# Cross-attention and expert layer in float32 parts: x's normed rows turned by VectorE blocks and GpSimd DMAs instead of TensorE, both query products late in the batch

## The chip, the cores and the metric

One core of a Trainium2 chip runs the kernel. The metric is the device time of one execution in microseconds; the median of several runs is given. A profiled execution is one more run, with its own time.

## What is computed

For each of 8 batches, x has 512 rows of 256 and the context 1601 rows of 256. The first layer is a cross-attention whose scores go through a sigmoid, not a softmax:

```python
q = (layernorm(x) @ Wq.T).reshape(B, L, 16, 16) * 16 ** -0.5
k = (ctx @ Wk.T).reshape(B, -1, 16, 16)
v = (ctx @ Wv.T).reshape(B, -1, 16, 16)
scores = sigmoid(einsum('blhd,bshd->bhls', q, k))
x = x + einsum('bhls,bshd->blhd', scores, v).reshape(B, L, 256) @ Wo.T
```

The second is a feed-forward layer on layernorm(x): a gate picks, for each of 16 experts and each batch, the 64 rows with the highest gate weights; these go through the expert's gated unit and are added to their rows, and a shared expert runs on all rows.

## The kernel before

**Attention, batch by batch.** A batch has 16 heads, 512 queries and 13 tiles of 128 keys. Its work is cut into 4 quarters (two halves of the heads, two sets of four heads in each) of 13 key tiles: 52 quads a batch. A quad is two *score pairs* (`scores`, L1735: two matmuls of 48 rows by 512 queries into one of three score banks), each followed by one sigmoid over 1024 columns on ScalarE (L876), and one *weighted sum* (`weighted_sum`, L1765). The 48 rows of keys and queries are three copies of 16 (high and low parts of float32 numbers), stacked in the tiles `keys` and `queries`.

**Products beside the scores.** While batch b's scores run, the products for batch c = b + 1 are made: keys K (`key_product`, by half of the heads and chunk of 512 keys), values V, queries Q (`query_halves`, one for each half), and, for batch b - 1, the output product O and the gate product G. T are the two products that turn x's normed rows by TensorE transposes (`turned_halves`, L1594), after which VectorE copies them into the tiles `nt_hi` and `nt_lo` (`turned_rows`, L1161) that Q reads. A product takes one of the three score banks (G has a bank of its own), like a score pair.

**The order** on TensorE is written out by hand: the strings `OPENING` (batch 0), `EACH` (batches 1 to 6) and `CLOSING` (batch 7) give S (score pair), W (weighted sum) and T (the next entry of the list `beside(b)`). VectorE and SyncE walk through the same list. On VectorE, `beside_quad(b, q)` (L1275) puts further work after given quads q: x's layer norm for c (sums at 15, scale at 17, rows at 19), the norm of the residual rows of batch b - 1 at 12 and the split of the turned ones at 22.

**The way of the residual rows** (batch b - 1) to their turned parts does not go over TensorE: `turn_norm` (L1189) transposes 32x32 blocks of `norm` into `norm_blocks` in one VectorE instruction, `place_norm` (L759) on GpSimd's queue issues 16 DMAs that put the blocks in their places, into `norm` again, and `split_norm` (L1194) makes `nt_hi` and `nt_lo` of them. G reads the placed rows from `norm`.

**SyncE's queue** (L596 on, in the order of the list). After each key product: `write_keys` to DRAM. After the last key product of c, K of half 1, chunk 3: `stack_keys` for the first two quarters of c, twice six DMAs of 200 KB back from DRAM (L505), once the writes have landed. After Q of half 0: `stack_queries(c, 0)`, twelve DMAs of 64 KB from `query_parts` into `queries` (L522). At the first pair of the next batch: `stack_queries` of half 1, and the keys of the third quarter. After the second T: `load_x` for the batch after c (L538). The first score pair of a batch waits for all twelve DMAs of half 0 (`wait_queries`, L1756).

**GpSimd's queue** (L768): for each batch its four context loads (`load_ctx`), each when the buffer of two loads before has been split, and `place_norm`.

After the attention come 24 units of the feed-forward layer, which the diff does not touch, apart from six early products (U) beside batch 7's scores.

## Time and profile before

| | |
|---|---|
| median of 3 runs | 1309.55 us (1308.88 to 1310.62) |
| profiled execution | 1305.85 us |
| its span, first to last instruction | 1304.0 us |
| TensorE clock granted over the span | 0.999 of full |
| engines busy | TensorE 98%, ScalarE 76%, VectorE 56%, GpSimd 22% |
| attention batches (first sigmoid to next first) | batch 0 112.87 us, batch 4 109.08 us |

Line numbers (L876) are those of the kernel before. PE is TensorE, PEld its weight loads, DVE VectorE, ACT ScalarE, POOL GpSimd, SP SyncE; SPq and the like are an engine's instruction queue. Times are microseconds from the span's start, unless they are marked ns. The last column of most views tells how long the engine was idle just before, and what ended that.

### The profile page before, as it was taken

What the parts mean: (1) busy time and instruction counts of PE and PEld (TensorE: products, weight loads), DVE (VectorE), ACT (ScalarE), POOL (GpSimd) and SP (SyncE); (2) the same over time, 40 slices, a digit from 0 to 9 for tenths busy, and PEclk for the clock granted to TensorE, in tenths of its full rate; (3) what the DMA queues carried; (4) which work ended last, traced back from release to release, by engine and by line L of the source; (5) the groups of instructions that cost most, each with busy time, mean ns of one, the idle gap of its engine ahead of it and who ended that gap; (6) DMA issues with size and microseconds to landing.
All of it is one profiled execution on the core that took longest, in us unless ns stands there. A gap on an engine that the chain in (4) does not pass through costs nothing.

```text
span 1304.0 us, 25503 instructions
## 1 busy us (share of the span) xinstructions
PE 1283.8 (98%) x10200; PEld 772.1 (59%) x10200; DVE 732.5 (56%) x1377; ACT 985.3 (76%) x1148; POOL 286.9 (22%) x288
## 2 busy tenths in 40 slices
PE   8999999999999999999999999999999999999997
PEld 6445444444454544544444443336888888888887
DVE  6564475365266448437536633215558777777773
ACT  5888989998998899899999989996333455555553
POOL 3000030020002003002000200500001567677635
PEclk9999999999999999999999999999999999999999
DMA  7785973874776597387477549713543577777754
GB/s 215 179 188 126 139 184 111 125 162 133 130 139 166 118 137 171 113 131 148 149 129 140 127 93 156 169 34 114 195 130 110 181 201 192 188 192 190 192 109 49
DMA packets 118726, 190.82 MB, mean 146 GB/s; under 512 B 22448, under 2 KB 71600, under 8 KB 118608
## 3 DMA queue, kind: packets, MB, share of 16 engines
q1 hardware_dynamic: 98768, 155.21, 51.9%
q0 software_dynamic: 19648, 33.72, 12.4%
q8 instruction: 81, 1.33, 0.5%
q10 hardware_dynamic: 192, 0.26, 0.1%
q14 instruction: 37, 0.30, 0.1%
HBM read 108.43 MB, written 55.61 MB: 126 GB/s over the span
## 4 chain that ended last, share of the span: by engine, by line
PE 87%; issue 5%; DMA 2%; DVE 2%; ACT 2%; POOL 1%; SPq 0%; POOLq 0%; DVEq 0%; ACTq 0%
PE score L1839 19%; PE score L1751 18%; PE acc L1780 14%; PE misc L1780 13%; PE score L1857 9%; PE score L1566 5%; PE score L1580 5%; PE score L1589 2%; ACT probs L876 1%; PE score L1619 1%; PE score L1607 1%; DMA key_scr<-key_parts 1%; POOL norm L765 1%; DMA norm<-norm_blocks 1%; DMA ctx_raw<-ctx_t 1%
## 5 line engine op out<-in xcount | busy, mean ns | idle before, releaser
L876 ACT ACTIVATE probs<-score 128x1024 f32<-128x1024 f32 (+1 forms) x832 | 789.8, 1026 | 77.3 <-PE score L1751 70.6
L1751 PE MATMUL score<-queries,keys 48*128 48x512 f32 (+1 forms) x1664 | 312.2, 438 | 6.5 <-ACT probs L876 4.2
L1751 PEld LDWEIGHTS score<-queries,keys 48*128 48x128 f32 (+1 forms) x1664 | 139.1, 180 | 275.0 <-ACT probs L876 212.7
L1780 PE MATMUL acc<-probs,values 128*32 128x512 f32 (+1 forms) x1664 | 210.5, 601 | 0.0
L1780 PE MATMUL misc<-probs,values 128*32 128x512 f32 (+1 forms) x1664 | 205.8, 600 | 0.0
L1026 DVE TENSOR_REDUCE whole<-score 128x512 f32<-128x1024 f32 (+1 forms) x75 | 77.0, 1026 | 196.6 <-PE score L1566 119.6
L729 POOL DMA_DIRECT2D ctx_raw<-ctx_t x32 | 23.4, 733 | 642.6 <-DVE ctx_lo L1004 557.9
L801 POOL DMA_INDIRECT gathered<-norm_scr,gather_row x64 | 81.2, 1269 | 227.5 <-DVE gather_row L1374 212.2
L891 ACT ACTIVATE gelu<-score 128x512 f32<-128x512 f32 (+1 forms) x97 | 55.5, 580 | 84.6 <-PE score L1839 84.0
L814 POOL DMA_INDIRECT out<-result,add_row x64 | 106.6, 1666 | 48.4 <-ACT result L944 25.9
L1839 PE MATMUL score<-tok_hi,gu_hi 128*128 128x512 f32 (+1 forms) x388 | 117.0, 383 | 0.0
L1839 PE MATMUL score<-tok_lo,gu_hi 128*128 128x512 f32 (+1 forms) x388 | 116.2, 381 | 0.0
L1839 PE MATMUL score<-tok_hi,gu_lo 128*128 128x512 f32 (+1 forms) x388 | 116.2, 381 | 0.0
L1321 DVE TENSOR_TENSOR hidden<-gelu,score 128x512 f32<-128x512 f32 (+1 forms) x97 | 64.0, 664 | 92.6 <-PE score L1839 62.3
L899 ACT ACTIVATE hid_hi<-hidden 128x512 fp32r<-128x512 f32 (+1 forms) x100 | 61.0, 613 | 63.9 <-DVE hidden L1321 60.7
L1066 DVE TENSOR_REDUCE values<-score 128x512 f32<-128x1024 f32 (+1 forms) x52 | 59.3, 1141 | 71.7 <-PE score L1580 71.0
L1780 PEld LDWEIGHTS misc<-probs,values 128*32 128x32 f32 (+1 forms) x1664 | 40.7, 108 | 87.0 <-issue 76.6
L1780 PEld LDWEIGHTS acc<-probs,values 128*32 128x32 f32 (+1 forms) x1664 | 38.8, 108 | 77.0 <-issue 71.5
L1839 PEld LDWEIGHTS score<-tok_lo,gu_hi 128*128 128x128 f32 x388 | 71.8, 188 | 14.2
L1839 PEld LDWEIGHTS score<-tok_hi,gu_lo 128*128 128x128 f32 x388 | 71.8, 188 | 14.1
L1839 PEld LDWEIGHTS score<-tok_hi,gu_hi 128*128 128x128 f32 x388 | 70.2, 189 | 12.9 <-issue 0.8
L944 ACT ACTIVATE result<-score,add_w 128x256 f32<-128x256 f32 x60 | 23.6, 474 | 67.9 <-DVE add_w L1364 64.7
(257 smaller groups left out, 1626.2 us busy)
## 6 DMA issues: line engine op xcount, KB each, us to landing
keys<-key_scr SPq DMA_DIRECT2D x180, 200.2 KB, 8.0
key_scr<-key_parts SPq DMA_DIRECT2D x45, 512.0 KB, 8.3
gu_raw<-w_gu SPq DMA_DIRECT2D x17, 1024.0 KB
ctx_raw<-ctx_t POOLq DMA_DIRECT2D x24, 512.0 KB, 5.1
queries<-query_parts SPq DMA_DIRECT2D x186, 64.0 KB, 2.5
d_raw<-w_d SPq DMA_DIRECT2D x17, 512.0 KB
norm<-xn SPq DMA_DIRECT2D x224, 32.0 KB
xn<-x SPq DMA_DIRECT2D x8, 512.0 KB, 3.8
```

What stands on the lines that cost most here:

```text
L801: pool.indirect_dma_start(gathered[par][:, t, :], None, norm_scr[:, :], bass.IndirectOffsetOnAxis(ap=gather_row[par][:, t:t + 1], axis=0)) ...
L814: pool.indirect_dma_start(out[:, :], bass.IndirectOffsetOnAxis(ap=add_row[par][:, t:t + 1], axis=0), result[par][:, t, :], None, compute_o ...
L876: act.activation(probs[0:rows, (n + 1) % RING, 2 * pair:2 * pair + 2, :], score[SLOT[k]][0:rows, :, :], ACT.Sigmoid, scale=SCALE).then_inc ...
L899: act.activation(hid_hi[par][:, of, cols], hidden[:, f % 2, cols], ACT.Copy).then_inc(hid_hi_done, 1)
L1026: dve.tensor_reduce(whole[:, 0:n], score[SLOT[task]][:, :, 0:n].rearrange("p e s -> p s e"), AX_X, ALU.add).then_inc(halves_added, 1)
L1321: dve.tensor_tensor(hidden[:, f % 2, cols], gelu[:, f % 2, cols], of, ALU.mult).then_inc(hidden_done, 1)
L1566: mm = pe.matmul(bank[:, e, 0:n], W2[a][rows, WK, k, P * half:P * (half + 1)], parts_of_ctx(b, kc)[c][rows, k, 0:n], start=(j == 0 and k = ...
L1580: mm = pe.matmul(bank[0:n, e, D * i:D * (i + 1)], parts_of_ctx(b, kc)[a][rows, k, s0:s0 + n], W2[c][rows, WV, k, :], start=(j == 0 and k = ...
L1751: mm = pe.matmul(score[SLOT[k]][0:rows, g, :], keys[quarter % KEY_RING][of, pair, P * st:P * st + rows], queries[half][of, e, pair, :], st ...
L1780: mm = pe.matmul(sums_bank[n // NST % 2][32 * c:32 * (c + 1), :], values[b % 2][0:rows, st, half, c, :], probs[0:rows, (n + 1) % RING, c, ...
L1839: mm = pe.matmul(bank[:, f % 2, cols], (gu_hi, gu_lo)[a][slot][:, w, k, P * of:P * (of + 1)], (tok_hi, tok_lo)[b][par][:, k, cols], start= ...
L1857: mm = pe.matmul(d_bank[:, t2, D * (t % 2):D * (t % 2 + 1)], (hid_hi, hid_lo)[a][par][:, f, P * t:P * (t + 1)], (d_hi, d_lo)[b][slot][:, f ...
```

## The change

- T is gone, with `turned_halves`, `turned_rows` and their waits; batch 0's own two stay.
- x's normed rows of batch c are turned as the residual rows are: `turn_x` is one VectorE block transpose from `xn` into the tile `norm` (viewed as `x_blocks`), right after G has been copied out (in batch 0 after quad 30); `place_x` on GpSimd's queue puts the blocks into `xn` (viewed as `x_raw`) with 16 DMAs; `split_x` on VectorE makes `nt_hi` and `nt_lo` after quad 42 (batch 0: 40). Q waits for the split.
- GpSimd's queue is rearranged: `place_x(b)` stands after the first two context loads of the batch after it and before the third.
- SyncE loads the x of the next batch but one after Q of half 0 instead of after T.
- The list `beside` and the strings have a new order. The number of score pairs of the batch that stand before a product, in batches 1 to 6 (c = b + 1, half or chunk behind it):

| product | before | after | | product | before | after |
|---|---|---|---|---|---|---|
| T, first and second | 52, 60 | gone | | V chunk 2, two halves | 75, 78 | 68, 74 |
| V chunk 1, two halves | 44, 47 | 47, 50 | | K chunk 3, half 0 and 1 | 83, 83 | 79, 79 |
| K chunk 2, half 0 and 1 | 66, 72 | 59, 62 | | V chunk 3 | 86 | 80 |
| G of batch b - 1 | 70 | 72 | | Q half 0 (Q0), half 1 (Q1) | 63, 95 | 89, 92 |

In batch 0 the last K moves from 85 to 78, and Q0 from 68 to 86; Q1 stays at 95.

```diff
     if c < B:
         out += [("V", c, 0, 0), ("V", c, 0, 1),
                 ("K", c, 0, 1), ("K", c, 1, 1), ("V", c, 1, 0), ("V", c, 1, 1),
-                ("T", c, 0), ("T", c, 1), ("Q", c, 0), ("K", c, 0, 2)]
+                ("K", c, 0, 2), ("K", c, 1, 2), ("V", c, 2, 0)]
...
     if c < B:
-        out += [("K", c, 1, 2), ("V", c, 2, 0), ("V", c, 2, 1),
-                ("K", c, 0, 3), ("K", c, 1, 3), ("V", c, 3, 0), ("Q", c, 1)]
+        out += [("V", c, 2, 1), ("K", c, 0, 3), ("K", c, 1, 3), ("V", c, 3, 0), ("Q", c, 0), ("Q", c, 1)]
...
-EACH = ("SSWWSSTSWSSSWWSTSTSSWWSSTSSWSSSWWSSTSSWSSSWWSSTSWSSSWWSTSTSSWWSSSWWSSSWWSSTSWSSTSWSSSWWSTS"
-        "WSSSWWSSSWWSTSWSSTSWSSTSWSSSWTWSSTSWSSTSWSSTSWSSSWWSTTSSWSTSWSSSWWSSSWWSSTSWSSSWWSSSWWSS")
+EACH = ("SWWSSTSWSSSWWSTSTSSWWSSTSSWSSTSWSSTSWSSSWWSSSWWSSTSWSSSWWSSSWWSSTSWSSSWWSSSWWSSTSWSSTSWSSS"
+        "WWSSSWWSSTSWSSTSWSSSWWSSTSSWSSWTSSTSWSSSWWSTTSTSWSSSWWSSSWWSSTSWSSTSWSSSWWSSSWWSSSWWSS")
...
+        x_raw = xn[:].rearrange("p t d -> p (t d)").rearrange("p (k s) -> p k s", s=S)
+        x_blocks = norm[:].rearrange("p t d -> p (t d)").rearrange("p (j c) -> p j c", c=P)
...
             def load_x(b):
-                sp.wait_ge(misc_copied, COUNT["T", b - 1, KC - 1])
+                if b > 1:
+                    sp.wait_ge(x_split, b - 1)
+                else:
+                    sp.wait_ge(misc_copied, COUNT["T", 0, KC - 1])
                 sp.dma_start(xn[:], x_rows[b]).then_inc(x_in, 16)
...
                         elif task[0] == "Q":
                             if task[1] == 0 or task[2] == 0:
                                 stack_queries(*task[1:])
-                        elif task[0] == "T" and task[2] == KC - 1 and task[1] + 1 < B:
-                            load_x(task[1] + 1)
+                            if task[1] and task[2] == 0 and task[1] + 1 < B:
+                                load_x(task[1] + 1)
...
+            def place_x(b):
+
+                pool.wait_ge(x_turned, b)
+                for i in range(BLOCKS):
+                    for j in range(BLOCKS):
+                        pool.dma_start(x_raw[TURN * j:TURN * (j + 1), :, P * i:P * (i + 1)],
+                                       x_blocks[TURN * i:TURN * (i + 1), j::BLOCKS, :]).then_inc(x_placed, 16)
+
+            for kc in range(NCH - 1):
+                load_ctx(1, kc)
             for b in range(1, B):
-                for kc in range(NCH):
-                    load_ctx(b, kc)
+                load_ctx(b, NCH - 1)
                 if b >= 2:
                     place_norm(b - 2)
+                if b + 1 < B:
+                    load_ctx(b + 1, 0)
+                    load_ctx(b + 1, 1)
+                place_x(b)
+                if b + 1 < B:
+                    load_ctx(b + 1, 2)
...
+            def turn_x(b):
+                dve.wait_ge(xn_ready, b + 1)
+                if b == 1:
+                    dve.wait_ge(direct_written, 16 * len(DIRECT))
+                    dve.wait_ge(first_keys_in[1], STACK_DMAS)
+                else:
+                    dve.wait_ge(post_stored, STORE * (b - 1))
+                dve.transpose(x_blocks.rearrange("p j (t q) -> p t j q", q=TURN),
+                              xn[:].rearrange("p t (j q) -> p t j q", q=TURN)).then_inc(x_turned, 1)
+
+            def split_x(b):
+                wait_past(dve, nt_stored, STORE * (b - 1))
+                dve.wait_ge(x_placed, PLACE_DMAS * b)
+                for k in range(KC):
...
+                    dve.tensor_copy(hi, raw).then_inc(split_step, s.up())
+                    dve.wait_ge(split_step, s.now())
+                    last = dve.tensor_tensor(lo, raw, hi.bitcast(F32), ALU.subtract)
+                last.then_inc(x_split, 1)
...
+                if b == 0 and q == 30:
+                    turn_x(1)
+                if b + 1 < B and q == (40 if b == 0 else 42):
+                    split_x(b + 1)
...
                         copy_out(which)
+                        if which == ("G", b - 1) and b + 1 < B:
+                            turn_x(b + 1)
...
                 elif kind == "Q":
+                    if b:
+                        pe.wait_ge(x_split, b)
                     mm = query_halves(task[2], bank)
...
-                elif kind == "T":
-                    pe.wait_ge(xn_ready, b + 1)
-                    mm = turned_halves(xn, task[2], bank)
```

## Rows read from the trace of the kernel before

**Rows 1.** The page's first part: busy time and share of the span.

```profile
PE 1283.8 (98%) x10200; PEld 772.1 (59%) x10200; DVE 732.5 (56%) x1377; ACT 985.3 (76%) x1148; POOL 286.9 (22%) x288
```

**Rows 2.** Busy time by stretches: batches 0 and 4, first sigmoid to next first.

```profile
25.34:138.21 112.87, 111.55 (x1018) 55.44 (x1018) 60.36 (x105) 99.08 (x105) 3.61 (x5) 1.00 0.76 173
...
465.87:574.95 109.08, 108.36 (x984) 50.72 (x980) 58.77 (x119) 98.89 (x106) 11.40 (x20) 1.00 0.69 140
```

**Rows 3.** Timeline of ScalarE in batch 4: the sigmoids around both T and Q0.

```profile
522.51 10.79 ACT L876 ACTIVATE probs<-score 128x1024 f32<-128x1024 f32 x11 [0.30 <-PE score L1751]
533.73 2.89 ACT L876 ACTIVATE probs<-score 128x1024 f32<-128x1024 f32 x3 [0.43 <-PE score L1751]
```

**Rows 4.** Instructions by line and shape, to 950 us: T on TensorE and VectorE.

```profile
L1169 DVE CAST nt_hi<-score 128x256 fp32r<-128x256 f32 x28 | 10.6, 420 | 20.4 <-PE score L1597 19.2 <-DMA norm_t_scr<-nt_lo 1.2
...
L1597 PE MATMUL score<-ident,xn 64*128 64x64 f32 x112 | 5.7, 221 | 0.0
```

**Rows 5.** The same view: block transpose and low parts of the residual rows.

```profile
L1202 DVE TENSOR_TENSOR nt_lo<-norm,nt_hi 128x512 fp32r<-128x512 f32 x14 | 9.7, 692 | 0.5
...
L1191 DVE STREAM_TRANSPOSE norm_blocks<-norm 128x1024 f32<-128x1024 f32 x7 | 8.7, 1246 | 0.2
```

**Rows 6.** One line's instructions: the sixteen placing DMAs from 499.1 us.

```profile
L765 POOL DMA_DIRECT2D norm<-norm_blocks x16: 539/539/548, 499.1 to 507.1; - x16
...
DMA to landing us min/median/max: 6.1/8.0/9.1
```

**Rows 7.** Timelines of TensorE and VectorE: G, Q1 and batch 5's first pair.

```profile
538.25 0.62 PE L1649 MATMUL misc<-norm,gate 128*32 128x128 f32 x16
...
564.17 0.63 PE L1589 MATMUL score<-nt_hi,w_hi 64*128 64x512 f32 x4
...
574.20 0.50 PE L1751 MATMUL score<-queries,keys 48*128 48x512 f32 x2 [0.51 <-ACT probs L876]
...
538.93 0.29 DVE L1208 COPY gate_out<-misc 128x128 f32<-128x128 f32 x1 [1.09 <-PE misc L1649]
...
567.57 0.69 DVE L1034 TENSOR_TENSOR query_parts<-whole,query_parts 128x512 fp32r<-128x512 f32 x1
```

**Rows 8.** One line's DMAs: Q0's twelve from 534.5; the context load at 551.7.

```profile
L522 SPq DMA_DIRECT2D queries<-query_parts x12: 569/592/1237, 534.5 to 542.2; - x12
...
DMA to landing us min/median/max: 2.2/2.2/2.9
...
L729 POOL DMA_DIRECT2D ctx_raw<-ctx_t x1: 722/722/722, 551.7 to 551.7; - x1
...
DMA to landing us min/median/max: 4.8/4.8/4.8
```

**Rows 9.** Key reads, twelves: issues (SP), landings from 556.9, 447.0, 774.7, 122.1; DMA share.

```profile
556.88 7.56 SPq L505 DMA_DIRECT2D keys<-key_scr  x12
...
DMA to landing us min/median/max: 4.2/9.4/15.6
...
DMA to landing us min/median/max: 4.3/10.0/16.3
...
DMA to landing us min/median/max: 4.5/9.4/14.3
...
122.11 7.54 SPq L505 DMA_DIRECT2D keys<-key_scr  x12
...
DMA to landing us min/median/max: 4.1/9.3/14.8
...
558.00:576.00 18.00, 17.49 (x138) 6.22 (x138) 2.35 (x3) 17.14 (x20) 0.00 (x0) 1.00 1.02 135
```

**Rows 10.** Batch 0: SyncE's issues from 57.67; landings of its six reads and twelve query DMAs.

```profile
57.67 3.71 SPq L505 DMA_DIRECT2D keys<-key_scr  x6
61.43 7.59 SPq L522 DMA_DIRECT2D queries<-query_parts  x12
...
DMA to landing us min/median/max: 4.1/6.7/9.1
...
DMA to landing us min/median/max: 7.0/7.9/8.8
```

More of the change, by code:

```diff
@@ L407, in build @@
         norm_split = sem("norm_split")
+        x_turned = sem("x_turned")
+        x_placed = sem("x_placed")
+        x_split = sem("x_split")
         split_step = sem("split_step")
@@ L1159, in residual @@
                 dve.tensor_tensor(two, bank[:, 1, :], two, ALU.add).then_inc(misc_copied, 1)
-            def turned_rows(task):
-                k, by_half = task[2], "p (t e c) -> p e t c"
-                dve.wait_ge(misc_full, COUNT[task])
-                rows = score[SLOT[task]][:, :, 0:TT * ROWS].rearrange("p e (t c) -> p e t c", c=ROWS)
-                hi = nt_hi[:, k, :].rearrange(by_half, t=TT, e=2)
-                lo = nt_lo[:, k, :].rearrange(by_half, t=TT, e=2)
-                for e in range(2):
-                    last = dve.tensor_copy(hi[:, e], rows[:, e])
-                last.then_inc(split_step, s.up())
-                dve.wait_ge(split_step, s.now())
-                for e in range(2):
-                    last = dve.tensor_tensor(lo[:, e], rows[:, e], hi[:, e].bitcast(F32), ALU.subtract)
-                last.then_inc(misc_copied, 1)
+            def turn_x(b):
[11 more added lines that the diff above has]
+                for k in range(KC):
+                    raw = x_raw[:, k, :].rearrange("p (i t q) -> p t i q", i=BLOCKS, q=TURN)
+                    hi = nt_hi[:, k, :].rearrange("p (t i q) -> p t i q", i=BLOCKS, q=TURN)
+                    lo = nt_lo[:, k, :].rearrange("p (t i q) -> p t i q", i=BLOCKS, q=TURN)
+                    dve.tensor_copy(hi, raw).then_inc(split_step, s.up())
+                    dve.wait_ge(split_step, s.now())
+                    last = dve.tensor_tensor(lo, raw, hi.bitcast(F32), ALU.subtract)
+                last.then_inc(x_split, 1)
             def early_ups(task):
@@ L1225, in copy_out @@
                     k = task[2]
-                    if kind == "T" and k == 0:
-                        wait_past(dve, nt_stored, STORE * (b - 1))
-                    if kind == "T" and task not in FIRST:
-                        turned_rows(task)
-                    else:
-                        two_parts(task, nt_hi[:, k, :], nt_lo[:, k, :])
+                    two_parts(task, nt_hi[:, k, :], nt_lo[:, k, :])
                 if kind in "KV" and LAST_OF[b, task[3] if kind == "K" else task[2]] == task:
@@ L1592, in query_halves @@
                 return mm
-            def turned_halves(tile, k, bank):
-                for t in range(TT):
-                    for e, rows in enumerate(ROW_TILES):
-                        mm = pe.transpose(bank[:, e, ROWS * t:ROWS * (t + 1)], tile[rows, t, P * k:P * (k + 1)],
-                                          ident[rows, rows])
-                return mm
             def out_halves(b, t2, bank):
```

8 lines of the change are left out of this document (4 added, 4 removed).

## The prediction

> **What bounds the kernel now.** I read the page's first part, then the busy times batch by batch, then ScalarE's own timeline inside one batch, then the DMA queue of SyncE. Everything is set against the profiled execution, whose time is 1305.85 us with a span of 1304.0 us; the median of the runs shown is 1309.55 us, 3.7 us above it, and I add the change to the median at the end.
>
> TensorE looks full over the whole span, 98% [rows 1]. That is a mean over stages, so I read one attention batch. From the first sigmoid of batch 4 to the first of batch 5 are 109.08 us, ScalarE is busy for 98.89 of them and TensorE for 108.36 [rows 2]. TensorE's busy time has its waits for a free score bank inside, so neither figure alone names the bound. The timeline shows how they meet: ScalarE runs sigmoids back to back, and loses 0.30 to 0.43 us about once per extra product, because that product takes one of the three score banks [rows 3]. A batch is therefore one chain of scores and sigmoids; VectorE (58.77 us) and GpSimd (11.40 us) have room [rows 2]. What stops TensorE, which takes its work in a fixed order, stops ScalarE some 2 to 3 sigmoids later, and it is not made up, as there are only three banks.
>
> **What is removed.** Two turning products per batch, 14 in all: 112 transposes of some 221 ns, with 28 copies of 420 ns and as many subtractions on VectorE, which I take at the same [rows 4]. The VectorE work is off the chain. On the chain the turning of batch 4 costs what ScalarE waited after it: 0.30 us after the first one, and after the second nothing of its own, since the next gap, 0.43 us, lies 11 sigmoids later, behind the query product [rows 3]. I take 0.3 us a batch, with 0 and 2 x 0.43 = 0.86 us as its ends; 7 x 0.3 = 2 us gained. The other products are moved, not removed, and I take each to cost the same gap wherever it stands.
>
> **What is added on VectorE and GpSimd.** One block transpose per batch (1246 ns as for the residual rows), two copies of 420 ns and two subtractions of 692 ns: 1.25 + 2.22 = 3.5 us a batch, against the 8 x 0.42 = 3.4 us that go [rows 4, 5]. Covered by VectorE's idle 50 us; without that cover it would cost 0.1 us a batch. GpSimd issues 16 DMAs of 0.54 us, 8.5 us in one go [rows 6], covered by its idle time; behind them on its queue stands only the context load of the next batch, which is used half a batch later.
>
> The new rows' chain is long, so its end has to be placed. In batch 4 the gate product G starts at 538.25 with 70 score pairs before it; a pair's pitch is 109.08/104 = 1.05 us. In the new order 72 pairs stand before it, but the two turnings and Q0 no longer do (some 0.3 + 0.43 us): about 539.6. Copying G ends 0.97 us later (538.93 + 0.29 against 538.25 [rows 7]), the block transpose 1.25 us after that: 541.8. Sixteen issues end at 550.4; the last lands 2.2 us (the nearest quiet DMAs, the queries' [rows 8]) to 9.1 us (this very placing beside key reads [rows 6]) after its own issue, and the two splits take 2.3 us: 554 to 561. Q0 stands at pair 89, six pairs before Q1's old place at 564.17 [rows 7]: 564.2 - 6.3 - 0.7 = 557.2. So Q0 may wait between 0 and 4 us. I take 0, as only key writes and small transfers run beside it in mid-batch, which is nearer to the quiet row. As the next step shows, this wait would not be added anyway.
>
> **What is moved: the stacking of Q0 behind the keys.** This is the term that decides. Before, Q0's twelve DMAs are issued in mid-batch and land 2.2 to 2.9 us after issue [rows 8]. At the end of a batch SyncE issues twelve reads of keys, 200 KB each, as soon as the last key product is written out: 556.88 to 564.44. They keep all DMA engines at a share of 1.02 for 18 us, and the last lands 15.6 us after its issue, at 579.4, already in the next batch (its first sigmoid is at 574.95) [rows 2, 9]. That hurts nobody before: the next quarter's keys are the first six, and what is queued behind all twelve, the second half's queries, is used half a batch later. In the new order Q0 is at pair 89 and the last key product at pair 79, so SyncE issues Q0's twelve DMAs *after* the twelve key reads, on one queue. How such a pair of groups behaves the trace shows once, in batch 0: six key reads from 57.67, the last landing 60.8 + 9.1 = 69.9; twelve query DMAs from 61.43, the first landing only 8.8 us after issue at 70.2, the last at 68.43 + 7.0 = 75.4 [rows 10]. The queue is served in order, and twelve queued query DMAs take 75.4 - 69.9 = 5.5 us behind the last key read.
>
> The sum for a middle batch, on batch 4's clock. The first key read moves with the last key product from pair 83 to 79 and loses what no longer stands ahead of it: 556.88 - 4 x 1.05 - 0.7 = 552.0. Last key read: + 22.5 (579.4 - 556.88) = 574.5. Last query DMA: + 5.5 = 580.0. Q0's own chain is earlier: from 557.2, with 568.26 - 564.17 = 4.1 us from the product's start to its parts [rows 7], SyncE is free at 552.0 + 7.6 = 559.6, the twelve issues run from 561.3 to 568.9; even 4 us later they would be queued before the keys have drained. The first score pair of batch 5 waits for all twelve. Its sigmoid starts 574.95 - 574.20 = 0.75 us after the pair [rows 2, 7]: 580.75 instead of 574.95, **5.8 us more per batch**, less what is already counted (the 2 us gained sit inside the 552.0). Other groups of key reads land 14.3 and 16.3 us after their last issue, against 15.6 here [rows 9]: 4.5 to 6.5 us, 5.5 in the middle. Boundaries of this kind, at the ends of batches 1 to 6: 6 x 5.5 = 33 us (27 to 39).
>
> Out of batch 0 the last key product moves from pair 85 to 78, seven pairs of 112.87/104 = 1.085 us: 122.11 - 7.6 - 0.7 = 113.8; last key read + (129.1 + 14.8 - 122.1 = 21.8) = 135.6; queries + 5.5 = 141.1; sigmoid 141.9 against 138.21: 3.7 us [rows 2, 9]. Batch 7 has no queries to stack and stays. A context load, issued at 551.7 and landed 4.8 us later [rows 8], some 5 us ahead of the key reads, now follows GpSimd's sixteen issues (from 550.4) and is 1.6 us ahead of the first read: it may hold the reads up by nothing, or by all that it takes beyond a small DMA's 2.2 us, 2.6 us a batch. It is still ahead of them, so I take 0 and keep 6 x 2.6 = 16 us for the upper end. Sum: 33 + 3.7 = 37 us. 1305.85 + 37 = 1342.9 for a profiled execution; **1309.55 + 37 = 1346.5** for the median.
>
> Against this speaks a rule of the Trainium skill, page "DMA: Bandwidth & Descriptors", section "Anatomy of one DMA — SWDGE (gpsimd) path": about 2.0 us fixed plus the bytes at 436 GB/s. By it, as an estimate, a read of 200 KB would occupy the queue for 0.46 us, twelve for 5.5 us, the keys would be gone before Q0's DMAs are issued, and the sum would be -2 us. The trace has 1.6 us each ((579.4 - 556.88 - 4.2)/11), and the measurement decides.
>
> **Rivals.** *A, the queries come in time (faster).* If the key reads left room for others, Q0's DMAs would land 2.2 to 2.9 us after issue as in mid-batch [rows 8], by 571.8, before the first pair at 574.2 - 0.7 = 573.5, which is the point from which it holds. Then only the 2 us gained are left: 1307.5. For it: the key reads need 1.6 us each on engines that take a query DMA in under 0.5 us, so an engine free for a moment would do. Against it [rows 10]. (The page's rule above would bring this case.) Chance 0.11. *B, half a price.* The two groups share the engines, so that a query DMA overtakes keys in part; the last query lands near 577, +2.5 us a boundary, 1309.55 + 7 x 2.5 = 1327. Chance 0.09. *C, dearer.* The placing or the context load drag the key reads, or the rows come so late that Q0 misses the drained queue. The point is Q0's parts ready after 567 (the keys' end at 574.5 less 7.6 of issue); the context load alone gives up to 1346.5 + 16 = 1362.5. Chance 0.08. *D, no change:* a stall of 0.3 us that eats the gain; chance 0.02.
>
> **How the numbers follow.** The forecast, stalls of 4.5 to 6.5 us a boundary (1335 to 1352), has 0.70. The range must leave out no more than A, D and the dear half of C: 1324 to 1358. About 0.2%, 2.6 us, is what a measurement of this kernel can tell from no change. Slower by more than that: forecast, B and C, 0.87; within it: D and 0.04 of A, whose gain of 2 us, with 0 and 6 as its ends, falls on either side: 0.06; faster: the rest of A, 0.07.
>
> **What would show it.** In the changed kernel ScalarE should have one gap of 4 to 7 us before the first sigmoid of each of batches 1 to 7, with a period of some 115 us; SyncE's twelve query DMAs should be issued right behind twelve key reads and land 7 to 14 us after issue; TensorE's idle time should be ended by a query DMA and not by VectorE's split. The gaps at the old turning places should be gone. I am wrong if the batch period is 109 us or less, or if TensorE waits at Q0 (VectorE's split) for more than 4 us.

## The result, and the profile after

The changed kernel takes **1380.31 us** (median of 5 runs, 1377.04 to 1381.6) against 1308.92 us before on the same chip: a ratio of 1.054, 95% interval 1.0526 to 1.0553, some 71 us slower. The forecast was 1346.5, within 1324 to 1358. The direction is right, the size is little more than half of what came.

The first view is the page's first part; it answers to [rows 1].

```profile
PE 1298.1 (94%) x10088; PEld 770.0 (56%) x10088; DVE 741.6 (54%) x1356; ACT 985.5 (72%) x1148; POOL 352.3 (26%) x400
```

TensorE has 112 instructions fewer and its share of the span falls from 98% to 94%: it now stands idle, in a span of 1377.4 us. Where it does so, the groups by line show in two rows, of the score matmuls and of the sigmoids behind them: busy time, mean ns of one, idle time of the engine just before them, and who ended how much of it. First the changed kernel, then the kernel before:

```profile
L899 ACT ACTIVATE probs<-score 128x1024 f32<-128x1024 f32 (+1 forms) x832 | 791.0, 1027 | 147.6 <-PE score L1774 141.1
L1774 PE MATMUL score<-queries,keys 48*128 48x512 f32 (+1 forms) x1664 | 312.9, 441 | 58.5 <-DMA queries<-query_parts 43.6 <-DVE values L1089 10.1 <-DVE early_up L1212 2.6
```

```profile
L876 ACT ACTIVATE probs<-score 128x1024 f32<-128x1024 f32 (+1 forms) x832 | 789.8, 1026 | 77.3 <-PE score L1751 70.6
L1751 PE MATMUL score<-queries,keys 48*128 48x512 f32 (+1 forms) x1664 | 312.2, 438 | 6.5 <-ACT probs L876 4.2 <-DVE values L1066 0.7
```

ScalarE's idle time before its sigmoids grew by 147.6 - 77.3 = 70.3 us, nearly all of the 73.4 us by which the two profiled spans differ. On TensorE three new waits stand behind it: 43.6 us for the DMAs that stack the queries, 10.1 us for VectorE's value copies, 2.6 us for its copy of an early product. These rows are the measure for the experiments below.

The busy times batch by batch (stretch, its length; PE, PEld, DVE, ACT, POOL; granted clock, DMA share, GB/s), from first sigmoid to next first, and two short stretches at the end of batch 1:

```profile
25.51:140.25 114.74, 110.27 (x1000) 54.50 (x1002) 60.93 (x103) 98.92 (x106) 12.14 (x21) 1.00 0.82 179
...
499.06:618.69 119.63, 109.07 (x968) 50.85 (x964) 58.89 (x116) 98.87 (x106) 20.11 (x36) 0.97 0.66 133
618.69:739.47 120.78, 109.40 (x968) 50.15 (x972) 58.76 (x116) 99.07 (x104) 20.31 (x36) 0.97 0.67 131
...
253.00:256.20 3.20, 0.00 (x0) 0.00 (x0) 0.00 (x0) 1.32 (x2) 0.00 (x0) 1.00 1.06 138
256.20:263.00 6.80, 3.05 (x14) 0.91 (x18) 0.00 (x0) 1.02 (x1) 0.00 (x0) 0.50 1.10 182
```

Batches 1 to 6 take 117.6 to 120.8 us, against about 109.1 before [rows 2]; ScalarE's busy time is the same, some 99 us. The last row is news: while TensorE waits at the end of batch 1, its granted clock falls to 0.50, 1.2 GHz instead of 2.4, and stays there for 6.8 us, 3.7 of them the rest of the wait and 3.1 the work behind it. The same happens at each boundary but the one after batch 3, and behind some of the other waits. ScalarE's and TensorE's timelines at that boundary (start, duration, in brackets the idle time before):

```profile
249.66 4.66 ACT L899 ACTIVATE probs<-score 128x1024 f32<-128x1024 f32 x5
260.78 1.02 ACT L899 ACTIVATE probs<-score 128x1024 f32<-128x1024 f32 x1 [6.46 <-PE score L1774]
264.20 2.89 ACT L899 ACTIVATE probs<-score 128x1024 f32<-128x1024 f32 x3 [2.40 <-PE score L1774]
```

```profile
259.95 0.80 PE L1774 MATMUL score<-queries,keys 48*128 48x512 f32 x2 [7.40 <-DMA queries<-query_parts]
260.68 3.06 PE L1803 MATMUL misc<-probs,values 128*32 128x512 f32 x16
...
315.33 0.50 PE L1774 MATMUL score<-queries,keys 48*128 48x512 f32 x2 [1.64 <-DVE values L1089]
...
479.88 1.22 PE L1620 MATMUL score<-nt_hi,w_hi 64*128 64x512 f32 x4 [5.18 <-DVE nt_lo L1203]
```

ScalarE loses 6.46 us before the batch's first sigmoid, and 2.40 us more behind it. The second gap has two causes: the new string begins with one score pair and two weighted sums, so after a wait the next pair stands behind 16 matmuls, and these take 3.06 us at the low clock. Over all boundaries ScalarE's gaps before the first sigmoid are 3.06, 6.46, 7.12, none (batch 4), 7.38, 8.05 and 4.88, together 37.0; the second gaps are 2.93, 2.40, 2.57, 0.90, 2.64, 3.28 and 1.53, together 16.3 (before, the largest gap at these places is 0.41 or less).

SyncE's issues at the end of batch 4, and the landings of the twelve key reads and of the twelve query DMAs:

```profile
588.45 7.56 SPq L510 DMA_DIRECT2D keys<-key_scr  x12
598.50 7.56 SPq L527 DMA_DIRECT2D queries<-query_parts  x12
...
DMA to landing us min/median/max: 3.8/11.1/17.5
...
DMA to landing us min/median/max: 12.1/12.9/13.7
```

This is the row of DMAs that the prediction drew: the last key lands about 595.4 + 17.5 = 612.9, and the last query ends TensorE's wait at 617.86, 5 us behind it.

The other two places are VectorE's, in batches 2 and 3, and GpSimd's in batch 3:

```profile
311.92 0.43 DVE L1230 CAST nt_hi<-norm 128x512 fp32r<-128x512 f32 x1 [5.09 <-DMA norm<-norm_blocks]
...
314.06 1.22 DVE L1089 TENSOR_REDUCE values<-score 128x512 f32<-128x1024 f32 x1
317.26 1.23 DVE L1089 TENSOR_REDUCE values<-score 128x512 f32<-128x1024 f32 x1 [1.99 <-PE score L1611]
...
477.52 0.43 DVE L1201 CAST nt_hi<-xn 128x512 fp32r<-128x512 f32 x1 [5.63 <-DMA xn<-norm]
```

```profile
460.09 7.02 POOL L781 DMA_DIRECT2D xn<-norm  x13 [19.28 <-DVE norm L1191]
469.23 1.60 POOL L781 DMA_DIRECT2D xn<-norm  x3 [2.12 <-issue]
```

In batch 2 VectorE waits 5.09 us for the placing of the *residual* rows. The copy of a value product, ready at about 312.0 (TensorE's last matmul of it starts at 311.63), stands behind that wait and its four instructions, starts at 314.06, and the score pair that needs its bank waits 1.64 us. In batch 3 the placing of *x's* rows is late, and TensorE waits 5.18 us at Q0.

Batch 4 shows where VectorE's wait comes from. First VectorE before (block transpose of the residual rows, the first value copy, the split behind it), then in the changed kernel (block transpose, split, value copy):

```profile
493.72 1.25 DVE L1191 STREAM_TRANSPOSE norm_blocks<-norm 128x1024 f32<-128x1024 f32 x1
...
512.61 1.22 DVE L1066 TENSOR_REDUCE values<-score 128x512 f32<-128x1024 f32 x1 [2.30 <-PE score L1580]
513.76 0.42 DVE L1200 CAST nt_hi<-norm 128x512 fp32r<-128x512 f32 x1
```

```profile
529.02 1.25 DVE L1221 STREAM_TRANSPOSE norm_blocks<-norm 128x1024 f32<-128x1024 f32 x1
...
549.04 0.43 DVE L1230 CAST nt_hi<-norm 128x512 fp32r<-128x512 f32 x1 [5.44 <-DMA norm<-norm_blocks]
...
551.18 1.22 DVE L1089 TENSOR_REDUCE values<-score 128x512 f32<-128x1024 f32 x1
```

Two things changed. The value copy that stood ahead of the split stands behind it. And the rows come later: the block transpose starts 30.0 us into the batch instead of 27.9, and the split gets its rows 50.0 us into the batch; before, it found them in place at 47.9.

### The profile page after: what moved, and what is told of

Read it like the earlier page. It is cut to its first block and busy times, and to the rows that moved or that the text cites. A ratio compares the mean times of both kernels' runs of the same rounds, so it can differ in the third digit from the quotient of the medians.

```text
span 1377.4 us, 25377 instructions
## 1 busy us (share of the span) xinstructions
PE 1298.1 (94%) x10088; PEld 770.0 (56%) x10088; DVE 741.6 (54%) x1356; ACT 985.5 (72%) x1148; POOL 352.3 (26%) x400
## 5 line engine op out<-in xcount | busy, mean ns | idle before, releaser
L899 ACT ACTIVATE probs<-score 128x1024 f32<-128x1024 f32 (+1 forms) x832 | 791.0, 1027 | 147.6 <-PE score L1774 141.1
L1774 PE MATMUL score<-queries,keys 48*128 48x512 f32 (+1 forms) x1664 | 312.9, 441 | 58.5 <-DMA queries<-query_parts 43.6
L1803 PE MATMUL misc<-probs,values 128*32 128x512 f32 (+1 forms) x1664 | 218.0, 629 | 0.0
L837 POOL DMA_INDIRECT out<-result,add_row x64 | 110.3, 1723 | 46.4 <-ACT result L967 23.9
L1862 PE MATMUL score<-tok_hi,gu_hi 128*128 128x512 f32 (+1 forms) x388 | 117.6, 384 | 0.6 <-issue 0.2
L781 POOL DMA_DIRECT2D xn<-norm x112 | 60.3, 546 | 134.6 <-DVE norm L1191 132.0
```

The costliest lines, as they stand in the source:

```text
L781: pool.dma_start(x_raw[TURN * j:TURN * (j + 1), :, P * i:P * (i + 1)], x_blocks[TURN * i:TURN * (i + 1), j::BLOCKS, :]).then_inc(x_placed, 16)
L837: pool.indirect_dma_start(out[:, :], bass.IndirectOffsetOnAxis(ap=add_row[par][:, t:t + 1], axis=0), result[par][:, t, :], None, compute_o ...
L899: act.activation(probs[0:rows, (n + 1) % RING, 2 * pair:2 * pair + 2, :], score[SLOT[k]][0:rows, :, :], ACT.Sigmoid, scale=SCALE).then_inc ...
L1774: mm = pe.matmul(score[SLOT[k]][0:rows, g, :], keys[quarter % KEY_RING][of, pair, P * st:P * st + rows], queries[half][of, e, pair, :], st ...
L1803: mm = pe.matmul(sums_bank[n // NST % 2][32 * c:32 * (c + 1), :], values[b % 2][0:rows, st, half, c, :], probs[0:rows, (n + 1) % RING, c, ...
L1862: mm = pe.matmul(bank[:, f % 2, cols], (gu_hi, gu_lo)[a][slot][:, w, k, P * of:P * (of + 1)], (tok_hi, tok_lo)[b][par][:, k, cols], start= ...
```

## The experiments

Times are medians, each beside the kernel before on the same chip (1306.8 to 1309.0 us).

**1. The twelve key reads ahead of the queries.** In the changed kernel, the reads for the second quarter, which is 26 score pairs away, go behind Q0's query DMAs:

```diff
                         if task == ("K", b + 1, 1, NCH - 1):
                             stack_keys(4 * b + 4)
+                        if task == ("Q", b + 1, 0):
                             stack_keys(4 * b + 5)
```

> The changed kernel with one thing moved on SyncE's queue: the key reads of the second quarter of the next batch are issued after Q0's twelve query DMAs, not before. Theory T (order on the queue: seven waits of 4 to 9 us for queries behind twelve key reads, and the half clock and small waits that follow each): six key reads end some 9 us earlier, no wait above 1 us at the first pair of a batch, clock near 1.0 all through, period 109 to 110.5 us, 1306 to 1320 us. Rival R (the turned rows come late, so Q0 itself is late and the order of the DMAs behind it matters little): 1365 to 1380 us. The same batch's second quarter may miss its keys if they come too late: then a gap before pair 26.

Measured: 1325.18 us, 1.0136 (1.0087 to 1.0185), above the expected range, since the value copies' waits stay. The row of the score matmuls:

```profile
L1775 PE MATMUL score<-queries,keys 48*128 48x512 f32 (+1 forms) x1664 | 311.2, 438 | 15.5 <-DVE values L1090 8.7 <-DVE early_up L1213 2.2 <-ACT probs L900 2.1
```

The wait for queries is gone from it, and with it 71.4 - 18.4 = 53 us (each taken against its own runs of the kernel before). The value copies' idle time is still there (8.7 us).

**2. The same order of DMAs in the kernel before.** T stays, Q0 stays in mid-batch; only its stacking is issued behind the keys:

```diff
-                            if task[1] == 0 or task[2] == 0:
+                            if task[1] == 0:
                                 stack_queries(*task[1:])
...
                             stack_keys(4 * b + 5)
+                            stack_queries(b + 1, 0)
```

> The kernel before, with its transposes, its order and its early Q0, and only the twelve query DMAs of Q0 issued behind the twelve key reads. Theory T: the last query lands 5.5 us after the last key read, near 585 on batch 4's clock, so each of seven boundaries gets a wait of 10 to 11 us and the aftermath of 3 to 4 us: 1385 to 1425 us. Rival R (late rows are the cause): nothing is late here, 1309 us as before.

Measured: 1396.53 us, 1.0694 (1.0635 to 1.0753).

```profile
L1752 PE MATMUL score<-queries,keys 48*128 48x512 f32 (+1 forms) x1664 | 316.3, 444 | 77.8 <-DMA queries<-query_parts 72.6 <-DVE early_up L1183 1.8 <-DVE values L1067 1.0
```

Here Q0 had been made in mid-batch, and the wait is larger still, 9 to 12.3 us a boundary. So it is the place of the DMAs behind the keys, not a late Q0, that costs. With the last key product still at pair 83 the reads also start later: 93.7 us into batch 4 here, 89.4 us in the changed kernel.

**3. The query DMAs on GpSimd's queue.** The changed kernel, with Q0's twelve DMAs issued there, behind the placing, with a semaphore of their own:

```diff
+                pool.wait_ge(misc_copied, COUNT["Q", b, 0])
+                wait_past(pool, scores_done, GROUPS * (4 * (b - 1) + 2))
+                for j, part in enumerate(QUERY_PART):
...
+                            pool.dma_start(queries[0][ROWS * g + HD * j:ROWS * g + HD * (j + 1), e, :, :].bitcast(F32),
...
+                                           .bitcast(F32)).then_inc(queries_late, 16)
```

> The changed kernel with Q0's twelve query DMAs issued from GpSimd's queue, behind its placing and its context load, all else as changed. Theory T (order within SyncE's queue): they run beside the key reads, land 3 to 10 us after issue, and the wait at the first pair shrinks to 0 to 4 us: 1312 to 1350 us. Rival B (the DMA engines are full whatever the order, so that the queries end when the keys have drained): 1372 to 1385 us, with the last query still near the last key read.

Measured: 1388.24 us, 1.0618 (1.0565 to 1.067), a little above what the rival says; the cure that would follow from a queue served in order did not come. At the end of batch 3: GpSimd's issues; landings of the queries and, from 472.60, of the twelve keys; the load of the DMA engines.

```profile
483.25 5.99 POOL L805 DMA_DIRECT2D queries<-query_parts  x12 [9.45 <-DVE query_parts L1069]
...
DMA to landing us min/median/max: 13.6/14.6/15.3
...
DMA to landing us min/median/max: 4.1/11.8/19.8
...
484.00:504.00 20.00, 10.03 (x78) 2.97 (x74) 2.09 (x3) 11.29 (x13) 5.24 (x11) 0.88 1.04 138
```

On a queue of their own the queries still land only with the last keys or behind them (the first at 483.25 + 13.6 = 496.9 or later, the last when TensorE's wait ends at 504.15; the last key lands about 479.6 + 19.8 = 499.4). The engines are busy at a share of 1.04 throughout. The Trainium skill, page "DMA: Bandwidth & Descriptors", section "Issuing engines are not separate DMA queues", says that whichever engine issues, the DMAs run on the same 16 engines and interleave. The trace agrees: the first query lands some 2.5 us before the last key, and the last one behind it. So "one queue is served in order" was too narrow: on SyncE's queue and on GpSimd's alike, most of the bytes of the key reads went through first.

**4. What the low clock costs.** The changed kernel keeps TensorE busy with 30 useless products (14 out of batch 0) into the free bank just before the wait:

```diff
+                    if st == 0 and half == 0 and e == 0 and b:
+                        wait_slot(k)
+                        for _ in range(14 if b == 1 else 30):
+                            pe.matmul(score[SLOT[k]][:, 0, :], w_hi[:, WQ, 0, 0:P],
...
```

> The changed kernel with matmuls of no use (30 of 128x512, 14 at the first boundary) put into the free score bank just before the wait for the queries. Theory T, with the half clock as a cost of its own: the waits for queries stay, the granted clock stays at 1.0 after them, and the gap after the first sigmoid of a batch (2.4 to 3.3 us) shrinks to about 1 us: 1355 to 1368 us. Rival (the clock costs nothing, as ScalarE is the bound after a wait): 1377 to 1383 us.

Measured: 1375.77 us, 1.0527 (1.0475 to 1.0578): by the intervals no different from the change's 1.054, and less of a gain than expected. At the same boundary as above, and the clock there:

```profile
258.43 1.02 ACT L899 ACTIVATE probs<-score 128x1024 f32<-128x1024 f32 x1 [6.47 <-PE score L1779]
260.71 2.90 ACT L899 ACTIVATE probs<-score 128x1024 f32<-128x1024 f32 x3 [1.25 <-PE score L1779]
```

```profile
252.00:258.40 6.40, 5.90 (x30) 4.40 (x32) 0.00 (x0) 0.00 (x0) 0.00 (x0) 1.00 1.10 189
```

The clock stays at 1.00, and the second gap is 1.25 instead of 2.40 us. The total is blurred by the filler itself: at the start of batch 4, where the changed kernel waits 0.74 us, it adds a gap of 5.85 us. The same filler in the kernel of experiment 2, at every boundary:

```diff
+                    if st == 0 and half == 0 and e == 0 and b:
+                        wait_slot(k)
+                        for _ in range(36):
...
```

> The kernel of e2 (before, query DMAs behind the key reads), with 36 matmuls of no use just before each of the seven waits for queries. Theory T2 (the half clock behind a wait costs 2 to 3 us a boundary): the waits for queries end as in e2, the clock stays at 1.0 and the second gap of a batch (2.0 to 2.8 us in e2) goes: 1375 to 1385 us. Rival (the clock costs nothing): 1394 to 1398 us.

Measured: 1390.21 us, 1.0635 (1.06 to 1.067), again less of a gain than expected. At the ends of batches 0, 1 and 6 the filler ran out 5.9, 2.5 and 3.3 us before the queries landed, and the clock fell to 0.50 all the same. At the other four it ran out 1.6 to 2.8 us before, and the clock stayed at 1.00. ScalarE at the end of batch 3, without the filler (experiment 2) and with it:

```profile
519.04 2.88 ACT L877 ACTIVATE probs<-score 128x1024 f32<-128x1024 f32 x3 [2.75 <-PE score L1752]
```

```profile
517.60 2.90 ACT L877 ACTIVATE probs<-score 128x1024 f32<-128x1024 f32 x3 [0.58 <-PE score L1757]
```

At the four boundaries that kept the clock the second gap is 0.57 to 0.58 us, against 2.48 to 2.79 without the filler: there the low clock costs 1.9 to 2.2 us a boundary. The batches that begin and end at such a boundary (3, 4 and 5) took 119.60, 118.87 and 118.42 us against 122.20, 122.06 and 120.88, but these differences hold those of the waits for queries too.

**5. The split of the residual rows.** The changed kernel, with this split three quads later on VectorE, and nothing else:

```diff
-                if b and q == 22:
+                if b and q == (25 if b + 1 < B else 22):
                     split_norm(b - 1)
```

> The changed kernel, key reads first as in the change, with the split of the residual rows after quad 25 alone. Theory T3: the key reads and the queries behind them keep their length, so each batch still ends with its wait; but the first key read comes as much earlier as VectorE's wait near pair 49 held up, some 2 to 4 us a batch: 1350 to 1370 us. Rival (that wait is hidden behind the wait for the queries): 1376 to 1382 us.

Measured: 1363.33 us, 1.0417 (1.0389 to 1.0446), 17 us less than the change.

```profile
L1774 PE MATMUL score<-queries,keys 48*128 48x512 f32 (+1 forms) x1664 | 311.7, 440 | 46.1 <-DMA queries<-query_parts 43.2 <-DVE early_up L1212 0.8 <-ACT probs L899 0.2
```

```profile
548.22 1.22 DVE L1089 TENSOR_REDUCE values<-score 128x512 f32<-128x1024 f32 x1 [5.28 <-PE score L1611]
551.51 1.23 DVE L1089 TENSOR_REDUCE values<-score 128x512 f32<-128x1024 f32 x1 [2.06 <-PE score L1611]
...
554.98 0.42 DVE L1230 CAST nt_hi<-norm 128x512 fp32r<-128x512 f32 x1
```

The 10.1 us for the value copies are gone from the row, those for queries are as before. Both value copies now run as soon as their product is there, and the split finds its rows in place. In the kernel before, the first value product stood at pair 44, so its copy was ahead of the split after quad 22, and the placing landed while VectorE waited for that product and copied it (512.61 and 513.76 above). The change put the product at pair 47, behind the split, and the rows come some 2 us later. How much of the wait is the order and how much the late rows was not tried apart; the late split takes away both.

Could the kernel before have had the late split too? After quad 24 there:

```diff
-                if b and q == 22:
+                if b and q == (24 if b + 1 < B else 22):
                     split_norm(b - 1)
```

> The kernel before with only the split of the residual rows moved from after quad 22 to after quad 24, as far as T leaves room. If the 1.3 us a batch that e7 gains on the kernel before comes from that split alone: 1299 to 1303 us. If T stands in its way (T writes the tiles that the split has filled and waits for their store): VectorE waits for the store at T, 1308 to 1330 us.

Measured: 1371.71 us, 1.0469 (1.0447 to 1.0491), dearer than either expectation. TensorE and VectorE in batch 4:

```profile
559.16 1.22 PE L1751 MATMUL score<-queries,keys 48*128 48x512 f32 x4 [6.88 <-DVE nt_lo L1173]
```

```profile
557.56 0.76 DVE L1169 CAST nt_hi<-score 128x256 fp32r<-128x256 f32 x2 [6.03 <-DMA norm_t_scr<-nt_lo]
```

No: T's copies go into the same tile `nt_hi`, which must first have been written out; the copies of T's first product, at pair 52, wait for that, and the score pair behind it waits for them. It is T's removal that makes room for the late split.

**6. Both edits together, and nothing else.**

```diff
+                        if task == ("Q", b + 1, 0):
                             stack_keys(4 * b + 5)
...
-                if b and q == 22:
+                if b and q == (25 if b + 1 < B else 22):
```

> The changed kernel with two edits and nothing else: the key reads of the second quarter issued behind Q0's query DMAs (as in e1), and the split of the residual rows after quad 25 instead of 22 (as in e11). Theory: the two costs lie in different places and add up, so that the late split takes from e1 what it took from the changed kernel and from e6, 14 to 17 us: 1325.2 - 14 to 17 = 1308 to 1311 against 1306.8 to 1309 before, ratio 1.001 to 1.004; a period of some 108 us in batches 1, 2, 4, 5 and 6, batch 3 some 115 with its wait at Q0. Rival: the fifteen spare DMAs or the old order of batch 7 in the version that was faster than before did more than e5 and e6 showed of them (5.4 us together); then the two edits alone stay above 1313 us. Second rival: those two parts did nothing, and e1's run was only on a slower chip; then 1305 to 1307, ratio 0.997 to 0.999.

Measured: 1309.41 us (12 runs), 1.0003 (0.9985 to 1.0022). The sigmoids and the score matmuls, then batches 3, 4 and 7, and GpSimd in batch 3:

```profile
L900 ACT ACTIVATE probs<-score 128x1024 f32<-128x1024 f32 (+1 forms) x832 | 789.4, 1027 | 78.2 <-PE score L1775 72.0
L1775 PE MATMUL score<-queries,keys 48*128 48x512 f32 (+1 forms) x1664 | 308.3, 436 | 4.8 <-DVE early_up L1213 1.4 <-ACT probs L900 0.9
```

```profile
354.31:468.39 114.08, 109.01 (x968) 51.05 (x964) 59.05 (x116) 98.83 (x106) 20.22 (x36) 0.99 0.69 140
468.39:576.16 107.77, 107.41 (x968) 49.99 (x964) 58.87 (x116) 98.70 (x106) 20.14 (x36) 1.00 0.68 145
...
791.76:893.23 101.47, 98.72 (x772) 36.33 (x772) 24.10 (x48) 97.84 (x105) 18.33 (x20) 1.00 0.51 107
```

```profile
440.04 1.61 POOL L782 DMA_DIRECT2D xn<-norm  x3 [2.10 <-issue]
```

The four kernels, each as the difference to the kernel before on its chip, give the shares of the two causes:

| | all twelve reads ahead | six behind the queries | difference |
|---|---|---|---|
| split after quad 22 | +71.4 | +18.4 | 53.0 |
| split after quad 25 | +54.4 | +0.9 | 53.5 |
| difference | 17.0 | 17.5 | |

They add up, though the intervals of the ratios leave each figure uncertain by 2 to 7 us. ScalarE's idle time, from one profiled execution each, says the same: 147.6, 93.0, 132.3 and 78.2 us (in the order of the table), so 54.6 and 54.1 us for the key reads, 15.3 and 14.8 for the split. Of the split's share not all is the split: batch 7, where that edit changes nothing, is 3.9 us shorter in this kernel than in experiment 1 (101.47 against 105.36); it has no stretch at the low clock, and in experiment 1 it has one of 6.8 us.

**7. What is left, and a version that is faster.** Batch 3 still takes 114.08 us, with 4.71 us at Q0, and batch 7 stays above its 99.41 us of before; its string has an early product (U) two pairs earlier. Fifteen small DMAs on GpSimd's queue in batch 0, added to experiment 1, were to move the break in its issues:

```diff
+            for i in range(15):
+                pool.dma_start(spare[0:1, 4 * i:4 * i + 4], x[0:1, 4 * i:4 * i + 4]).then_inc(spare_in, 16)
```

> The kernel of e1 with 15 DMAs of 16 bytes put on GpSimd's queue in batch 0. In all five kernels so far that have it inside a row of placings, GpSimd's 134th DMA is issued 0.6 to 2.4 us late, and in the changed kernel it lies in the placing of the rows that end batch 3, whose Q0 then waits 4.9 to 5.2 us. Theory T2 (it is the count of DMAs on that queue): the late issue moves to a context load, batch 3 loses its wait at Q0, and the time falls by 5 to 8 us against e1's 1325: 1317 to 1320 us. Rival (something of batch 3 itself, or of that moment, is late): the wait stays where it is, 1323 to 1327 us.

Measured: 1320.65 us, 1.0091 (1.006 to 1.0123), not clear of experiment 1 by the intervals. The break stays in the same placing, one DMA later (14 and 2 instead of 13 and 3), and the wait at Q0 with it (4.31 us). But it isn't tied to batch 3, as two other kernels show, the one before (batch 7) and that of experiment 3 (batch 2):

```profile
829.52 6.90 POOL L765 DMA_DIRECT2D norm<-norm_blocks  x13 [0.61 <-issue]
```

```profile
370.50 2.00 POOL L805 DMA_DIRECT2D queries<-query_parts  x4 [2.06 <-issue]
```

In all ten kernels without spare DMAs the break stands before the 134th DMA that GpSimd issues, in the four with them before the 150th. So it goes with the place in GpSimd's row of DMAs; but fifteen more in front moved it by sixteen, so a plain count of DMAs isn't the whole rule. Then the string of batch 7 as it was before:

```diff
-CLOSING = ("SSSWWSSSWWSSTSSWSSSWWSSTSSWSSWSSWSSWSSWWSSSWWSSWSSWSSWSSWSSWSSWSSWSSWSWSSWSSWSTSSWSSSWWSSS"
...
+CLOSING = ("SSSWWSSSWWSSSWWSSTSSWSSSWWSSTSSWSSWSSWSSWSSWSWSSWSSWSSWSSWSWSSWSSWSSWSWSSWSSWSSWSTSSWSSTSS"
...
```

> e5, and batch 7's order as before the change (the string CLOSING alone). Theory T2: the first early product U then stands at pair 52, not 50; its copy does not wait for pair 51 while TensorE waits for its bank, and the half clock of 6.8 us behind that goes: batch 7 falls from 105.4 to 99.5 us, 5 to 6 us less than e5. Rival (batch 7 is longer since everything before it is later): within 1 us of e5.

Measured: 1319.77 us, 1.0081 (1.0053 to 1.0108); 0.9 us less, which the runs can't tell from nothing. In both, batch 7 took 101.5 and 100.3 us with no low clock in it, against 105.4 in experiment 1 with one: most of what batch 7 lost there goes together with the clock, and not with the string, which the kernel with the spare DMAs alone still has. Then the late split on top:

```diff
-                if b and q == 22:
+                if b and q == (25 if b + 1 < B else 22):
```

> e6, and the split of the residual rows after quad 25 instead of 22 in batches 1 to 6, behind both value products of pairs 47 and 50. Theory T2 (VectorE waits there for the placing, and the two values behind it on its queue hold a score bank): the waits of 0.7 to 2.4 us near pair 49 go, 3 to 6 us less than e6, near the kernel before: 1304 to 1310 us. Rival (the wait moves to the next product behind the split): within 1 us of e6.

Measured: **1305.39 us, 0.9974 (0.9956 to 0.9992)**, 14 us less than without the late split, more than expected, and here batch 7 is the same in both (100.4 and 100.3 us); faster than the kernel before by a quarter of a per cent. The same with spare DMAs over all 128 partitions:

```diff
-                pool.dma_start(spare[0:1, 4 * i:4 * i + 4], x[0:1, 4 * i:4 * i + 4]).then_inc(spare_in, 16)
+                pool.dma_start(spare[:, 4 * i:4 * i + 4], x[0:P, 4 * i:4 * i + 4]).then_inc(spare_in, 16)
```

> The kernel of e7 with its 15 spare DMAs widened from one partition to 128 (16 bytes each). In e5 the late issue on GpSimd's queue did not leave the placing that ends batch 3: it only moved on by one DMA, so that DMAs of one partition did not count. Theory T3 (what counts is DMAs that are spread over all engines): with 15 such the late issue falls on a context load, batch 3 keeps the period of its neighbours, 107.8 us instead of 114.6: 1297 to 1301 us. Rival (it belongs to batch 3 or to that moment): 1303 to 1308 us, the wait at Q0 as in e7.

Measured: 1305.60 us, 0.9975 (0.9964 to 0.9986). The break stands where it was, with 4.77 us at Q0, so it makes no difference to it whether a spare DMA goes to one partition or to 128; the gain is found a second time. Which part of this version takes it below experiment 6 (the spare DMAs or the old string; 3 us between two intervals that touch) is not settled.

## Why the prediction was wrong in size

**The term that decided held.** Stacking behind twelve key reads was taken at 33 us for six boundaries and 3.7 out of batch 0, 37 together; ScalarE's gaps before the first sigmoids sum to 37.0, and TensorE's wait to 43.6, or 40 without the 0.5 us a boundary that the first pair waited for anyway [rows 7]. The agreement is partly luck. Four boundaries cost 6.5 to 8.1 us, more than the 5.8 drawn, two less (3.1 out of batch 0, 4.9 after batch 6), and the one after batch 3 nothing, since there the wait had been spent at Q0. And two slips cancel in part: at the end of batch 4 the last query ended the wait 118.8 us into the batch instead of 114.1 (first key read at 89.4 instead of 86.1, and 24.4 instead of 22.5 us for the twelve), but TensorE also reached the wait at 110.5 instead of 107.6. The row of landings came as drawn: 12.1 to 13.7 us after issue (said: 7 to 14), 5 us behind the last key (5.5). Experiments 1 and 2 show the cause by taking it away and by putting it alone into the kernel before. Rivals A and B fall with that. The twelve reads took 24.4 us from first issue to last landing. The rate of the Trainium skill, page "DMA: Bandwidth & Descriptors", section "Anatomy of one DMA — SWDGE (gpsimd) path", would have had them through in 5.5 us, an estimate; the section gives it for DMAs that GpSimd issues, and these are SyncE's.

**Missing: what follows the wait.** The sum of a boundary ended with the step "Its sigmoid starts 574.95 - 574.20 = 0.75 us after the pair"; what the next pairs lose was put at nothing without a reason. ScalarE loses 16.3 us more behind the first sigmoids: one part because the string begins with one pair and two weighted sums (1.25 us a boundary even at full clock, experiment 4), the rest because TensorE came out of the wait at 1.2 GHz. Of the 16.3 us some 2.6 (0.4 a boundary) stand in experiment 1 too, so that 37.0 + 13.7 = 50.7 us are explained of the 53.0 and 53.5 us that the table of experiment 6 gives for the reads. The Trainium skill, page "TensorE: Matmul & The Clock Gate", section "Why this matters for your kernels", warns that idle gaps between matmuls bring the clock down; the trace has 0.50 at six of the seven boundaries, all but the one where the wait was 0.74 us. The kernel before, with a clock of 0.999, could not show it.

**Failed: "I take each to cost the same gap wherever it stands".** The moved value products were priced on TensorE alone. On VectorE one of them passed from before to behind the residual rows' split, which waits for a placing; what was queued behind that wait was not asked, nor that the rows would come later, with other work now ahead of their norm (in batch 4 a second copy of an earlier value product and a context split, at 521.70 and 522.85, stand ahead of it; before they stood behind it, at 495.05 and 496.19). TensorE's direct waits for it are 10.1 us; all in all the late split took 17 us off the changed kernel, 11 of them in batches 0 to 6 and 5 in batch 7, whose low clock went too, and 15 off the kernel of experiment 7, all in the batches before the last. So 11 to 15 us are the split's; the rest lies in batch 7 and goes together with the low clock there.

**Failed once: Q0's wait.** "Between 0 and 4 us, I take 0" held in batches 1, 2, 4, 5 and 6; in batch 3 it was 5.18 us, one of the two signs of being wrong that the prediction named. It adds nothing to the changed kernel's time, as the prediction argued (it took the place of the wait at the boundary), but stands alone once the keys are behind (batch 3 in experiment 6: 114.08 against 107.8).

**Too small: T.** Taken at 0.3 us a batch with 0.86 as the upper end. With both costs gone, batches 4, 5 and 6 take 107.77 to 107.83 us against 108.97 to 109.08 before: 1.2 to 1.3 us, though that holds the whole new order, and T alone wasn't taken out. T was priced by the gaps that ScalarE shows, on the reading that TensorE's busy time holds waits for a bank. The rows fit another reading: in the middle of a batch TensorE has next to no idle time (busy 108.36 of 109.08 us before, 107.41 of 107.77 in experiment 6), so T costs its own time there, 5.7 / 7 = 0.8 us a batch [rows 4]; the other 0.5 us is the wait of a batch's first pair [rows 7], which experiment 6 doesn't have (what ScalarE ends of these matmuls' idle time falls from 4.2 to 0.9 us). **Small:** batch 7, said to stay, lost 107.1 - 99.4 = 7.7 us, of which 2.1 remain in experiment 6; the low clock stood behind its wait for U. No run shows a cost of VectorE's and GpSimd's added work itself: experiment 6 has all of it and ends at +0.9 us.

**Open:** why GpSimd's issues break off at the 134th DMA, in the changed kernel inside batch 3's placing, and how much of that wait is the break and how much the key reads beside it. Whether the context load drags the key reads was not tried.

## What to carry to other kernels

When work moves, walk every queue it passes: the price of this change lay not in what it added but in two places where something was now queued behind a wait, twelve DMAs of 64 KB behind 2.4 MB that were not urgent, and two copies behind a split that waited for its rows. Order transfers by when they are needed; with the DMA engines full, another engine's queue brought no relief here. And price a stall of TensorE with what follows it: the clock it comes back with, and how many instructions stand between it and the next work of the engine that it feeds.

## What the runs showed of the hardware that was not expected

- TensorE came out of its waits of 5.81 to 8.98 us at five boundaries with a granted clock of 0.50, and fell to it 0.4 us behind the one of 4.27 us. It fell behind some shorter ones too (2.00 us at 552.45, low from 553.14), but not behind others of the same length (2.05 us at 195.75, 2.13 us at 673.99). Sixteen weighted-sum matmuls behind a wait took 3.06 us in the changed kernel and 1.92 us where filler had kept the clock up (experiment 4, at 502.41).
- GpSimd's issues of DMAs broke off for 0.6 to 2.4 us before the 134th DMA that it issues, in all ten kernels without spare DMAs, whatever the DMA belonged to (829.5 us before, 469.2 us in the changed kernel, 370.5 us in experiment 3). With fifteen spare DMAs in front the break was 1.8 us and stood before the 150th.
- Twelve query DMAs on GpSimd's queue landed 13.6 to 15.3 us after issue beside full DMA engines (experiment 3, end of batch 3), against 2.2 to 4.5 us on SyncE's in experiment 6, with six of the key reads moved behind them (end of batch 4).
